# Where the low part of the input is made, and what the projections of layers 0 and 1 wait for

## The reference

```
layer 0: q, k = Wq x + bq, Wk x + bk  (32 rows each);  v = Wv x + bv  (256 rows)
         out = gamma * (v softmax(q^T k)^T) + x;  then batch norm over all batches and positions
layer 1: xn = group_norm(x);  q, k, v = 256 rows each of W xn + b
         x + proj(softmax(q k^T / 16) v)
layers 2, 3: group norm, attention with 8 heads of 32 channels, projection, residual
```

## Time and profile before

| | us |
|---|---|
| median of 3 runs | 1897.23 |
| the three runs | 1895.79, 1897.23, 1905.48 |
| profiled execution | 1903.71 |
| its span, first to last instruction | 1901.6 |
| layer 0 (0 to about 250) | 250 |
| layer 1 (to about 572) | 322 |
| layers 2 and 3 (to the end) | 1329.6 |
| busy over the span: PE, DVE, POOL, ACT | 1707.0, 1099.5, 1010.4, 928.7 |

### The profile page before, as it was taken

The page is one execution under the profiler, slowest core; times in us unless marked ns, Lnnn a source line. Parts: engine busy times, 40 slices in busy tenths (PEclk is TensorE's granted clock), DMA queues, the critical chain, the costliest instruction groups (busy, mean ns, idle before and its releaser), DMA issues.

```text
span 1901.6 us, 24881 instructions
## 1 busy us (share of the span) xinstructions
PE 1707.0 (90%) x8222; PEld 1007.7 (53%) x8222; DVE 1099.5 (58%) x1571; ACT 928.7 (49%) x1487; POOL 1010.4 (53%) x402
## 2 busy tenths in 40 slices
PE   3887959999992899999999998999999999999987
PEld 2666748888882454454444444445444444454422
DVE  2545535454432856765766667666675576666712
ACT  2433414343322165655565564565665656555553
POOL 2322312122103166775787585767776578757764
PEclk7989979999996698999999998999999999999988
DMA  3000000000001222021130230202202112032000
GB/s 137 17 17 17 1 1 1 1 1 1 1 1 32 56 68 67 1 68 45 25 67 1 67 84 1 67 20 54 67 2 67 42 49 67 2 90 68 1 23 22
DMA packets 24989, 67.44 MB, mean 35 GB/s; under 512 B 7200, under 2 KB 8992, under 8 KB 24864
## 3 DMA queue, kind: packets, MB, share of 16 engines
q1 hardware_dynamic: 24864, 65.78, 14.3%
HBM read 7.82 MB, written 4.19 MB: 6 GB/s over the span
## 4 chain that ended last, share of the span: by engine, by line
PE 50%; DVE 9%; issue 3%; ACT 3%; POOL 1%; DMA 1%; SPq 1%; DVEq 0%; POOLq 0%; ACTq 0%
PE psO L869 13%; PE psA L950 12%; PE psD L925 11%; PE psD L79 10%; DVE A L979 5%; PE psO L872 4%; DVE BNS L998 4%; ACT PR L1121 2%; POOL PA L1187 1%; DMA QS<-MROW 1%; SPq L1207 0%; ACT XH L1065 0%; SPq L1209 0%; DVE A L981 0%; DMA QS<-SL 0%
## 5 line engine op out<-in xcount | busy, mean ns | idle before, releaser
L1121 ACT ACTIVATE PR<-psA 128x512 f32<-128x512 f32 x1024 | 585.0, 597 | 520.3 <-PE psA L950 491.3
L998 DVE TENSOR_REDUCE BNS<-psD 128x1 f32<-128x512 f32 x1024 | 632.6, 685 | 241.5 <-PE psD L925 241.4
L1187 POOL TENSOR_TENSOR PA<-PA,PR 128x2048 f32<-128x2048 f32 x128 | 585.1, 4571 | 20.5 <-ACT PR L1121 9.3
L950 PE MATMUL psA<-QS,KS 97*128 97x512 f32 x1024 | 463.5, 461 | 39.1 <-ACT PR L1121 30.5
L925 PE MATMUL psD<-KS,QS 96*128 96x512 f32 x1024 | 419.2, 446 | 33.2 <-DVE BNS L998 17.8
L950 PEld LDWEIGHTS psA<-QS,KS 97*128 97x128 f32 x1024 | 194.2, 193 | 335.0 <-ACT PR L1121 180.0
L869 PE MATMUL psO<-PR,V 128*32 128x512 f32 x2048 | 273.3, 642 | 0.7 <-ACT PR L1121 0.7
L925 PEld LDWEIGHTS psD<-KS,QS 96*128 96x128 f32 x1024 | 204.2, 200 | 123.9 <-DVE BNS L998 80.2
L594 POOL TENSOR_SCALAR P<-P,RS 128x1024 f32<-128x1024 f32 x64 | 71.8, 1122 | 356.1 <-DVE RS L345 356.1
L1187 POOL TENSOR_TENSOR PA<-PR 128x2048 f32<-128x2048 f32 x32 | 146.0, 4564 | 134.9 <-ACT PR L1121 134.9
L979 DVE RECIPROCAL A<-psO 128x512 f32<-128x512 f32 x32 | 107.4, 3358 | 148.0 <-PE psO L872 148.0
(11 more groups left out here) (129 smaller groups left out, 1810.7 us busy)
## 6 DMA issues: line engine op xcount, KB each, us to landing
KS<-SH SPq DMA_DIRECT2D x128, 128.0 KB, 2.5
QS<-SH SPq DMA_DIRECT2D x128, 128.0 KB, 2.5
KS<-SL SPq DMA_DIRECT2D x64, 128.0 KB, 2.5
QS<-SL SPq DMA_DIRECT2D x64, 128.0 KB, 2.5
X<-x SPq DMA_DIRECT2D x4, 1024.0 KB, 7.6
out<-X SPq DMA_DIRECT2D x4, 1024.0 KB, 4.4
KH<-KL SPq DMA_DIRECT2D x8, 128.0 KB, 2.3
QH<-KL SPq DMA_DIRECT2D x8, 128.0 KB, 2.4
```

What stands on the lines that cost most here:

```text
L950: e.matmul(psA[:, s % 2, :], KS[0:STACK + 1, p, q, j * PART:(j + 1) * PART], QS[0:STACK + 1, p, q, h * HALF:(h + 1) * HALF], start=True, s ...
L998: top = e.tensor_reduce(MXH[:, h, q, tile:tile + 1], full, AX.X, ALU.max)
L1121: e.activation(PR[:, J % 4, (s % QUADH) * HALF:(s % QUADH + 1) * HALF], psA[:, s % 2, :], ACT.Exp, scale=scale).then_inc(exp_done, 1)
L1187: e.tensor_tensor(PA[:, :], PR[:, (J - 1) % 4, :] if j == 1 else PA[:, :], PR[:, J % 4, :], ALU.add).then_inc(sum_done, 1)
```

## The change

VectorE gets an `input_low` of its own. In layer 0 it makes every XL, in layer 1 only that of batch 0; it stands in VectorE's queue ahead of `low(0, 0)` at a layer's start, and in layer 0 at the end of row i = 4, behind PTL of row 4 and ahead of row 5's reciprocal of row 6, the row maximum of row 7 and PTL of row 5. GpSimd keeps `input_low` for the later batches of layer 1. `project` waits for XH at its start and for XL only ahead of the products WH XL of its first unit; for that the products are ordered by kind, then half of psD, then t. In layer 1 XH is computed by ScalarE from X with group norm's scale and bias, waiting for the batch norm in X (a new semaphore, `bn_done`), while XN is still made for XL.

```
 project:
-                                    e.wait_ge(xl_done, CT * (b + 1))
-                                for h in range(2):
-                                    mv = slice(h * HALF, (h + 1) * HALF)
-                                    mm = split_products(e, psD[0:width, slot, mv],
-                                                        [(ww[:, t, cols], xx[:, t, mv])
-                                                         for ww, xx in ((WH, XH), (WL, XH), (WH, XL)) for t in range(CT)])
+                                for k, (ww, xx) in enumerate(((WH, XH), (WL, XH), (WH, XL))):
+                                    if i == 0 and k == 2:
+                                        e.wait_ge(xl_done, CT * (b + 1))
+                                    for h in range(2):
+                                        mv = slice(h * HALF, (h + 1) * HALF)
+                                        for t in range(CT):
+                                            mm = e.matmul(psD[0:width, slot, mv], ww[:, t, cols], xx[:, t, mv],
+                                                          start=(k == t == 0), stop=(k == 2 and t == CT - 1))
 vector:
+                            def input_low(b):
+                                for t in range(CT):
+                                    e.wait_ge(xh_done, CT * b + t + 1)
+                                    if L1:
+                                        e.wait_ge(xn_done, CT * b + t + 1)
+                                    src = XN[:, t * N:(t + 1) * N] if L1 else X[:, b, t, :]
+                                    e.tensor_tensor(XL[:, t, :], src, XH[:, t, :].bitcast(F32), ALU.subtract).then_inc(xl_done, 1)
 normalise, batch norm in X:
-                                                    ALU.mult, ALU.add)
+                                                    ALU.mult, ALU.add).then_inc(bn_done, 1)
 vector, start of a layer:
+                            input_low(0)
                             for i in range(NQK):
                                 low(i, 0)
 vector, row i:
+                                    if not L1 and i == 4 and more:
+                                        input_low(b + 1)
 scalar, input_high:
                                     if L1:
-                                        e.wait_ge(xn_done, CT * b + t + 1)
-                                        src = XN[:, t * N:(t + 1) * N]
+                                        e.wait_ge(bn_done, CT * b + t + 1)
+                                        e.activation(XH[:, t, :], X[:, b, t, :], ACT.Identity, scale=SCB[:, t, b, 0:1],
+                                                     bias=SCB[:, t, b, 1:2]).then_inc(xh_done, 1)
                                     else:
                                         e.wait_ge(x_loaded[b], 16)
-                                        src = X[:, b, t, :]
+                                        e.activation(XH[:, t, :], X[:, b, t, :], ACT.Copy).then_inc(xh_done, 1)
 gpsimd:
-                            input_low(0)
-                                    if more and i == 4:
+                                    if L1 and more and i == 4:
                                         input_low(b + 1)
```

More of the change, by code:

```diff
@@ L146, in one_head @@
                     xn_done, xh_done, xl_done = sem("xn_done" + n), sem("xh_done" + n), sem("xl_done" + n)
+                    bn_done = sem("batch_normed" + n)
                     stacked, shifted = sem("stacked" + n), sem("x_shifted" + n)
@@ L493, in input_high @@
                                 for t in range(CT):
+                                    if b and t == 0:
+                                        e.wait_ge(unit_full, index["v", 1, b - 1] + 1)
                                     if L1:
-                                        e.wait_ge(xn_done, CT * b + t + 1)
-                                        src = XN[:, t * N:(t + 1) * N]
+                                        e.wait_ge(bn_done, CT * b + t + 1)
+                                        e.activation(XH[:, t, :], X[:, b, t, :], ACT.Identity, scale=SCB[:, t, b, 0:1],
+                                                     bias=SCB[:, t, b, 1:2]).then_inc(xh_done, 1)
                                     else:
                                         e.wait_ge(x_loaded[b], 16)
-                                        src = X[:, b, t, :]
-                                    if b and t == 0:
-                                        e.wait_ge(unit_full, index["v", 1, b - 1] + 1)
-                                    e.activation(XH[:, t, :], src, ACT.Copy).then_inc(xh_done, 1)
+                                        e.activation(XH[:, t, :], X[:, b, t, :], ACT.Copy).then_inc(xh_done, 1)
                             def high(i, b):
@@ L581, in input_low @@
                                     e.wait_ge(xh_done, CT * b + t + 1)
-                                    src = XN[:, t * N:(t + 1) * N] if L1 else X[:, b, t, :]
-                                    e.tensor_tensor(XL[:, t, :], src, XH[:, t, :].bitcast(F32), ALU.subtract).then_inc(xl_done, 1)
+                                    e.wait_ge(xn_done, CT * b + t + 1)
+                                    e.tensor_tensor(XL[:, t, :], XN[:, t * N:(t + 1) * N], XH[:, t, :].bitcast(F32),
+                                                    ALU.subtract).then_inc(xl_done, 1)
                             def shift(b):
```

## The result

The changed kernel takes 1874.24 us (median of 6 runs, 1869.68 to 1877.02), the kernel before 1897.67 (6 runs, 1895.06 to 1905.62). The ratio on record for the series is 0.9857, 95% interval 0.9839 to 0.9875; the two medians divided give 0.9877. So the gain is 23 us by the medians and 27 by the ratio. The forecast was 1877, range 1867 to 1888. The profiled execution took 1877.02 us with a span of 1875.2, 26.4 us less span than before (1901.6, of an execution 6 us above the median of before); in a second series the ratio was 0.9861 (0.9838 to 0.9884).

What follows compares the result with a forecast made beforehand. TensorE was taken to wait for GpSimd's XL in layers 0 and 1. Steps of 3.8 + 2.8 + 8.7 + 5.0 + 1.6 = 21.9 us, less 2, gave 20 us net: median 1877 us, range 1867 to 1888.

Steps and rivals of the forecast that it cites:

- Step 1: Start of layer 0: TensorE needs XH alone and never waits for XL, so KL and its chain come earlier; gain 3.8 us.
- Step 2: Layer 0, batch 0 to 1: projection starts without waiting for XL, KL then bound by row 7's exponent; gain 2.8 us.
- Step 3: Layer 0, batches 1 to 2 and 2 to 3: shorter wait, products at 2.4 GHz; gains 4.6 and 4.1, together 8.7 us.
- Step 4: Start of layer 1: XH made from X without waiting for XN, XL covered by eight products; gain 5.0 us.
- Step 5: Layer 1, later batches: XL stays on GpSimd but is waited for later; gain 1.6 us at batch 0 to 1, then 0.
- clock term: Deduction of 2 us from the summed steps, for low-clock stretches after waits dealt anew and stacking waits 1 us longer.
- Rival 1: Contention with GpSimd makes XL cost 2.5 us on VectorE wherever it moved; gain 11.6 us, 1886; chance 0.08.
- Rival 2: Layer 0 batch changes: displaced row maximum and PTL eat steps 2 and 3 whole; 10.4 us left, 1887; chance 0.05.
- Rival 3: Another wait ends with XL's, such as psD's half held by row 6; only 8.8 us left, 1888; chance 0.02.
- Rival 4: Layers 2 and 3: low-clock stretches dealt anew cancel the gain (1897) or make it slower (1907); chance 0.09.

Runs made afterwards that it cites:

- after_max: Changed kernel with VectorE's XL of the next batch in layer 0 moved behind the row maximum of row 7, ahead of PTL of row 5; ratio 0.9826.
- xh_only: Kernel before with only XH in layer 1 made by ScalarE from X; XL on GpSimd and the projection's waits as before; ratio 0.9987.
- busy_wait: Kernel before with 16 extra products of XH ahead of each layer's first projection unit of a batch, issued when XH is ready; ratio 0.9998.
- gpsimd_low: Changed kernel with every XL back on GpSimd; the new place of the wait and XH from X stay; ratio 0.9893.
- order_only: Kernel before with only the projection's wait for XL moved ahead of its products WH XL; XL stays on GpSimd; ratio 0.9884.
- both_busy: Changed kernel with GpSimd computing XL a second time in layer 0, batches 1 to 3, at the same moment as VectorE; ratio 0.9910.
- stack_two_queues: Changed kernel with four high-part stacking copies issued first, once KL is written, and two low-part copies issued from ScalarE's queue; ratio 0.9822.

## Why the prediction was right, and where it was off

**Prices.** XL on VectorE took 1.217 to 1.227 us in all ten cases; 1.2 was taken from the 128x1536 split. XH from X took 2.37 us for two.

**Step 1**, 3.8: KL 2.6 us earlier, and XH 1.17 later by the load; its own part 3.75. **Step 2**, 2.8: 5.7 less 2.6, 3.1. KL is bound by the exponent of row 7, as forecast (60.34 + 1.12 = 61.46, KL starts at 61.45), and after_max shows that this costs 0.7 us. **Step 3**, 4.6 and 4.1: 4.9 and 3.9, with the projections at 2.4 GHz (granted clock 1.00) after waits of 0.84 us, as said. Part of this was luck: the step took the clock at which a projection starts from the wait ahead of it, 2.98 us of products behind 3.73 us of wait, and xh_only had 5.39 behind the same wait. Behind waits of 0.84 us the clock was 1.00 in every kernel here. The waits for stacking grew to 2.5 us, not 3. **Step 4**, 5.0: the wait went from 12.21 to 7.19, 5.0. **Step 5**, 1.6: the wait of 1.57 us is gone. XL on GpSimd took 5.17 us for two beside XN instead of 4.71, and no product waited for it. The forecast of layer 0, shorter by about 15 us, came to 16.1; that of layer 1, about 6, to 9.2.

**The sum's clock term was mis-sized, with the wrong sign.** I wrote "I take off 2", above all for stretches of low clock "dealt anew". The five steps with their own measured sizes make 3.75 + 3.1 + 8.8 + 5.0 + 1.6 = 22.2 us, less 1.2 for the late load; the profile shows 26.4. The other 5.4 us are: 1.6 us between KL of batch 3 and the end of layer 0; 2.5 us in layer 1 between its first product and the second batch's, beyond the 1.57; 0.2 in the rest of layer 1; and 1.1 in the unedited layers. The first two, 4.1 us, go with a higher clock; the last does not, its clock and PE's busy time being as before. From KL of batch 3 to the end of layer 0 PE was busy for 61.18 us at a clock of 0.98 instead of 63.43 at 0.95. In layer 1 these windows show it, first before:

```profile
267.81:326.21 58.40, 54.21 (x265) 45.04 (x265) 28.30 (x31) 23.52 (x30) 11.56 (x9) 0.92 0.00 1
```

then the changed kernel:

```profile
246.74:301.11 54.37, 51.75 (x264) 43.40 (x265) 30.36 (x33) 24.01 (x30) 10.80 (x8) 0.96 0.00 1
```

Same products, PE 2.5 us less busy, granted clock 0.96 instead of 0.92: before, both the first projection and the first scores began at 1.2 GHz, in the changed kernel only the projection did. The second profile of the changed kernel repeats it (17.8 and 9.1 us for layers 0 and 1), but both are set against one profile of before. busy_wait puts the clock's part in layer 0 at 4.5 us, of which 3.1 are in the two projections that step 3 already counts (4.80 and 4.25 us of products down to 2.98); that leaves 1.4, near the 1.6 found here. That work in place of a wait can raise the clock is shown by busy_wait in layer 0; that every wait removed does so is not, since gpsimd_low and order_only differ by 5.6 us with the same waits. On the medians the gain was 23.4 us, between the forecast's 20 and the profile's 26: there the five steps, without taking anything off, miss by 1.5 us, so the size of the clock's gain stays open, but a loss of 2 us fits neither figure.

**Rivals.** Rival 1 (contention): didn't occur. GpSimd was idle beside XL on VectorE at the changes of batch and at the start of layer 1. At the start of layer 0 it was not idle, though I had said so: `shift` of the first half began at 11.71 us, beside the second XL, and it was `shift` that waited (1.91 us instead of 1.11), at no cost, as GpSimd then was idle for 13.5 us. both_busy shows that contention would have cost 7 to 9 us at the three changes of batch alone. The Trainium skill (GPSIMD Engine Reference, "Key points") says that GpSimd shares SBUF interfaces with VectorE and contends with VectorE's instructions of two SBUF inputs. In both_busy the trace agrees: the XL that came second took 3.42 us, the one that came first 1.23. Rival 2 (displaced row maximum): its place was real and its price 0.7 us a change, not 3 or 4; after_max won it back at two of the three. Rival 3: no wait stayed. Rival 4: layers 2 and 3 took 1328.8 us before and between 1321.0 (after_max) and 1328.0 us (stack_two_queues) in the profiles of all other kernels; they vary by 8 us with no edit in them, and in these profiles never came out slower than before. So 8 us of difference between two single profiles can lie in code that neither changed.

**Attribution.** The prediction treated the three parts as one. The runs show that the place of the wait gives 1.2% alone, and XH from X too little to measure by itself. VectorE's XL gives 0.3 to 0.4% on top by the ratios, which their intervals do not settle; the traces show 1.3 us at each of three changes of batch and 0.8 at the start, 0.25%.

## What to carry to other kernels

Before making a late operand faster, ask which product needs it first: ordering products by operand and waiting for each only at its own gave 1.2% here at no cost, of 1.4% for the whole change. Three ways to shorten one wait don't add, so price each on top of the others. When work moves to another engine's queue, look at what stands behind it there and ask which of the two someone waits for first; here moving XL behind the row maximum brought 0.7 us at two changes of batch and lost 0.3 at the one where TensorE did not wait for XH. Compare single profiles stage by stage, and don't read a difference of some us as the edit's before its clock is set beside it.

## What the runs showed of the hardware

VectorE and GpSimd, both with two inputs in SBUF, take turns: the one that comes second waits until the other's operation of 1.2 or 2.35 us is through (3.42 and 3.43 us measured), so VectorE's 1.22 us can cost 3.4. GpSimd's `shift`, with one large input, waited in the same way for VectorE's XL: 2.02 us in after_max (its first half, from 58.93 us, while XL ran to 59.96) instead of 1.12. GpSimd's two-input XL also stretched beside VectorE's one-input XN, 5.17 us for two instead of 4.71. A 128 KB copy issued from ScalarE's queue beside four of SyncE's landed 2.9 and 3.6 us after its issue, from SyncE's own queue 2.4. The granted clock of TensorE over the same instructions with the same waits was 0.96 in one execution and 1.00 in another, 5.6 us apart in 180; behind the same wait of 3.7 us the same twelve products took 2.98 us at 1.00 (before) and 5.39 at 0.50 (xh_only).
